# A gated linear attention block on one core: x rows at the head of the odd step, moments stored early, the second x split right behind the decays

## What is computed

```python
x = x + attention(layernorm(x))          # 16 heads of 64
x = x + (layernorm(x) @ CB.T) * (SCB / 127) + bias

# attention: q = elu(x Wq) + 1, k = elu(x Wk) + 1, v = x Wv, a = sigmoid(x Wa + ba + 2)
# per head, token after token:
S = a_t * S + outer(k_t, v_t);  z = a_t * z + k_t
out_t = (q_t @ S) / (q_t @ z + eps)      # then out @ Wo
```

## Time and profile before

| | |
|---|---|
| median of 3 runs | 2289.2 us (2288.9 to 2291.93) |
| the profiled execution | 2286.59 us, its span 2284.8 us |
| mean granted TensorE clock | 0.960 of full |
| PE busy | 2097.7 us (92% of the span) |
| DVE, ACT, POOL busy | 1457.7, 679.5, 307.7 us |

### The profile page before, as it was taken

How to read it: one execution, slowest core, us unless ns; L and a number is a source line. 1 busy time by engine, 2 the same in 40 slices (tenths; PEclk the granted TensorE clock), 3 DMA queues, 4 the chain that set the end, 5 groups by cost and what they waited for, 6 DMA issues and landing times. The chain is left out here.

```text
span 2284.8 us, 71079 instructions
## 1 busy us (share of the span) xinstructions
PE 2097.7 (92%) x28424; PEld 1800.9 (79%) x28424; DVE 1457.7 (64%) x3308; ACT 679.5 (30%) x1288; POOL 307.7 (13%) x367
## 2 busy tenths in 40 slices
PE   6898898899999998899999998999879999999999
PEld 5777787778888887788888887888768888888887
DVE  6566666676666766666667666666655555555554
ACT  4233333333333333333333333333421111111111
POOL 0121111111221111111211111112010000000000
PEclk9999999999999999999999999999989999999999
DMA  5323233333323233223222333233333333333332
GB/s 167 85 81 84 79 94 97 90 84 88 92 79 83 83 92 107 82 86 90 84 81 81 87 94 102 83 88 98 106 120 111 110 112 119 113 115 110 110 111 87
DMA packets 204592, 220.81 MB, mean 97 GB/s; under 512 B 31360, under 2 KB 146560, under 8 KB 204544
## 3 DMA queue, kind: packets, MB, share of 16 engines
q1 hardware_dynamic: 204544, 220.13, 31.6%
HBM read 168.59 MB, written 51.44 MB: 96 GB/s over the span
## 5 line engine op out<-in xcount | busy, mean ns | idle before, releaser
L1188 PE MATMUL G<-w_hi,xT_hi 128*128 128x512 f32 x1024 | 417.9, 408 | 6.0 <-DVE xT_lo L818 4.6
L1188 PE MATMUL G<-w_lo,xT_hi 128*128 128x512 f32 x1024 | 408.1, 399 | 0.0
L1188 PE MATMUL G<-w_hi,xT_lo 128*128 128x512 f32 x1024 | 405.3, 396 | 0.0
L1188 PE MATMUL G<-xT_hi,w_hi 128*128 128x256 f32 x1024 | 292.0, 285 | 28.4 <-DVE xT_lo L818 27.3
L1188 PE MATMUL G<-xT_lo,w_hi 128*128 128x256 f32 x1024 | 289.7, 283 | 0.0
L1188 PE MATMUL G<-xT_hi,w_lo 128*128 128x256 f32 x1024 | 289.7, 283 | 0.0
L682 ACT ACTIVATE relu_t<-G 128x512 f32<-128x512 f32 x256 | 152.7, 596 | 456.7 <-PE G L1188 456.7
L1188 PEld LDWEIGHTS G<-w_hi,xT_hi 128*128 128x128 f32 x1024 | 198.5, 194 | 50.5 <-DVE xT_lo L818 5.0
L1188 PEld LDWEIGHTS G<-w_hi,xT_lo 128*128 128x128 f32 x1024 | 197.3, 193 | 43.7
L1188 PEld LDWEIGHTS G<-xT_hi,w_hi 128*128 128x128 f32 x1024 | 196.1, 191 | 42.3 <-issue 41.1
L1188 PEld LDWEIGHTS G<-w_lo,xT_hi 128*128 128x128 f32 x1024 | 198.7, 194 | 36.9
(11 more groups left out here) (131 smaller groups left out, 3744.9 us busy)
## 6 DMA issues: line engine op xcount, KB each, us to landing
abc<-decay_rows SPq DMA_DIRECT2D x256, 128.0 KB, 3.1
pbc<-product_rows SPq DMA_DIRECT2D x256, 128.0 KB, 3.0
attn_rows<-attn SPq DMA_DIRECT2D x512, 64.0 KB, 2.0
at_rows<-attn_rows SPq DMA_DIRECT2D x64, 512.0 KB, 3.3
xt<-in_x SPq DMA_DIRECT2D x64, 256.0 KB, 2.7
x_in<-in_x SPq DMA_DIRECT2D x64, 256.0 KB, 3.4
out_rows<-xt SPq DMA_DIRECT2D x64, 256.0 KB, 2.0
xT_in<-in_xT SPq DMA_DIRECT2D x31, 512.0 KB, 5.0
```

The costliest lines, as they stand in the source:

```text
L1188: made = nc.tensor.matmul(to, lhs, rhs, start=(n == 0), stop=(n == len(passes) - 1))
```

## The change

On SP, `load_pair` is cut in two. `load_rows` (the two `xt` loads) stands at the head of the odd step, behind the first `abc` loads. `load_columns` (the `xT_in` load) stands behind the second `abc` loads of the odd step and ahead of the `pbc` loads. `spread_norm` is cut as well: `store_norm` stands at the head of the even step, and the rest of it (`bias_b`) ahead of the even step's `pbc` loads, with no wait between them but the store's own. On DVE, `x_lo(1)` stands right behind `decays()`, and `elu_k(1, 0)` ahead of `normalised(0)`, in both steps. In the written-out steps -1 and 0 the split of the fourth and fifth weight slabs (`split_hi(3)`, `split_lo(3)`, `split_lo(4)`), `chunk_decay`, and the first `x_stats` and `x_moments` change places.

```diff
-                def load_pair():
+                def load_rows():
 
                     for s in range(2):
                         later = row(sp, i + 3 + s)
...
                         sp.dma_start(xt[s][:, :], x_rows[bass.ds(later, C), :]).then_inc(x_loaded[s], 16)
+
+                def load_columns():
+
                     sp.wait_ge(xT_lo_ready[1], pairs[1])
                     sp.wait_ge(z_ready, pairs[1])
                     at = (pair + 2) * DM
...
+                def store_norm():
+
+                    sp.wait_ge(rstd_ready, pairs[1])
+                    sp.dma_start(norm_rows, moments[:, :, :].rearrange("p s a -> p (s a)")).then_inc(norm_stored, 16)
+
                 def spread_norm():
 
-                    sp.wait_ge(rstd_ready, pairs[1])
+                    sp.wait_ge(norm_stored, p16[0])
                     wait(sp, xT_normal, pairs[-1])
-                    sp.dma_start(norm_rows, moments[:, :, :].rearrange("p s a -> p (s a)")).then_inc(norm_stored, 16)
-                    sp.wait_ge(norm_stored, p16[0])
...
+                gates = b == 1 and exists(i + 1)
+                second = isinstance(i, int) and i == 0
                 if isinstance(i, int) and i == NC - 3:
                     output_weights()
+                if b == 0 and exists(i + 2) and not second:
+                    store_norm()
                 if exists(i):
                     spread_decays(1, this)
                 if b == 0 and exists(i + 1):
                     spread_decays(0, coming)
+                if b == 1 and exists(i + 3):
+                    load_rows()
                 if exists(i - 2):
                     store_rows(1, i - 2, one[-2])
-                if b == 1 and exists(i + 1):
+                if gates:
                     store_decays()
                     if not exists(i):
                         sp.wait_ge(w_lo_ready, KT)
                     spread_decays(0, coming)
...
+                    if exists(i + 3):
+                        load_columns()
+                if b == 0 and exists(i + 2):
+                    if second:
+                        store_norm()
+                    spread_norm()
...
                     spread_products(1, this)
                 if exists(i + 1):
                     spread_products(0, coming)
-                if b == 0 and exists(i + 2):
-                    spread_norm()
                 if exists(i - 1):
                     store_rows(0, i - 1, one[-1])
-                if b == 1 and exists(i + 3):
-                    load_pair()
...
                     q_parts(0)
+                    if not first:
+                        chunk_decay()
+                    q_parts(1)
                     if first:
                         split_hi(3)
-                    chunk_decay()
-                    q_parts(1)
+                        chunk_decay()
                     copy_v(0)
...
                 if gates and not first:
                     x_lo(0, pairs[1], xT_in[:, :, tokens(0)])
                     decays()
+                if second:
+                    x_stats(x16[1])
+                    dve.wait_ge(stats_ready, pairs[1])
+                    x_moments(pairs[1])
+                    split_lo(4)
+                if exists(i):
+                    if gates:
+                        x_lo(1, pairs[1], xT_in[:, :, tokens(1)])
+                    elu_k(1, 0)
                 if exists(i - 1):
                     normalised(0)
...
-                if second:
-                    split_lo(4)
                 if exists(i):
-                    elu_k(1, 0)
-                    if gates:
-                        x_lo(1, pairs[1], xT_in[:, :, tokens(1)])
                     decay_matrix(1)
...
                     elu_q(0, 0)
-                    if first:
-                        split_lo(3)
                     decay_matrix(0)
...
                     elu_q(1, 1)
+                    if first:
+                        split_lo(3)
```

More of the change, by code:

```diff
@@ L497, in step @@
                     spread_decays(0, coming)
-                wait(sp, qs_ready[1], one[-1] if exists(i - 1) else None)
-                wait(sp, qs_ready[0], one[0] if exists(i) else None)
-                wait(sp, pc_ready, one[0] if exists(i) else None)
+                    if exists(i + 3):
[4 more added lines that the diff above has]
+                    spread_norm()
+                if exists(i - 1):
+                    sp.wait_ge(qs_ready[1], one[-1])
                 if exists(i):
+                    sp.wait_ge(qs_ready[0], one[0])
+                    sp.wait_ge(pc_ready, one[0])
                     spread_products(1, this)
@@ L1060, in step @@
                     decay_matrix(0)
-                    if second:
-                        x_stats(x16[1])
-                        dve.wait_ge(stats_ready, pairs[1])
                     elu_q(3, 0)
-                    if second:
-                        x_moments(pairs[1])
                     elu_k(0, 1)
```

## The result

The changed kernel takes 2186.48 us (median of 4 runs, 2181.32 to 2187.88), the one before 2290.27 us on the same chip: a ratio of 0.954, 95% interval 0.9525 to 0.956. The forecast was 2178 us, inside whose range of 2138 to 2232 this lies; it came out 8.5 us short of the promised gain. The profiled execution is 2187.04 us, its span 2185.2; mean granted clock 0.989 instead of 0.960.

What follows compares the result with a forecast made beforehand. PE, 92% busy, was bound by waits on DVE, late because xt came late, and a low clock; 103.6 us from 28 pairs, 3.3 early and 3.8 prologue make 110.7 off 2286.6, plus 2.6 to the median: 2178, range 2138 to 2232.

Steps and rivals of the forecast that it cites:

- The sum: Even and odd step together: 45.2 us without waits plus 2.25 of waits, a pair of 47.5, 3.7 less than 51.2.
- `xt` at the head of the odd step: SP's two xt issues stand some 20 us earlier; DVE's 4.81 us idle goes, and q is bound by ACT's exp.
- The clock: Loop pairs: with 2.25 us in two smaller waits the granted clock stays 1.00, winning 1.8 us a pair.
- the rival of the low clock: Loop: the clock drops all the same, 1.8 us in each of 28 pairs come back, 2228 us; chance 0.13.
- kT ends last: Next even step's head: ACT's kT, not DVE's q, ends last; PE waits 1.5 us (1.2 to 1.95).
- The state wait: Even step's head, after the scores: state there at 862.05 us, PE ready at 861.3, a wait of 0.75.
- `xT_in` ahead of `pbc`: SP's odd step: the load delays pbc by 0.95 us, 0.65 of issue and 0.3 of bytes (0.65 to 1.4).
- The rival in which `pbc` stands behind all of the 512 KB: SP, after the decays: the DMA queue works on 512 KB first, pbc lands 4 us late, 2316 us; slower, chance 0.05.
- `x_lo(1)` behind the decays: DVE ends xT_lo by 846.4 us, before PE needs it at 847.26; PE's wait of 0.92 us is won.
- Moments earlier: POOL's operations move some 10 us ahead; PE's first-pair wait of 6.27 us goes, weight splits lose 2.5, prologue wins 3.8.
- that rival: DVE's even step: POOL's operations slow it until q or k is late, 1 us a pair, 2206 us; chance 0.05.
- The early pairs and the tail: Outside the steady loop: two early pairs, without low clock, gain 1.6 us each; other pairs counted at the loop's 3.7.

Runs made afterwards that it cites:

- e2: The kernel before, with only the two xt loads moved to the head of the odd step: 2156.93 us, ratio 0.9426.
- e7b: The changed kernel with xT_in's load behind the odd step's last stores and an unused 2 KB load in its old place: 2164.28 us, ratio 0.9452.
- e3: The changed kernel with x_lo(1) and k on DVE put back behind the normalisation: 2174.53 us, ratio 0.9501.
- e5b: The kernel before, with only x_lo(1) and k on DVE moved ahead of the normalisation: 2297.11 us, ratio 1.0029.
- e8b: The kernel before, with only the change's reordering on ACT and DVE in the written-out steps -1 and 0: 2285.02 us, ratio 0.9976.
- e4: The changed kernel with the moments stored and loaded back behind the even step's pbc loads: 2184.05 us, ratio 0.9548.
- the 13 kernels: The kernel before, the changed kernel, and all follow-up variants of either; profiled spans from 2117.0 to 2294.8 us.
- after: The changed kernel itself, with all parts of the change, against the kernel before: 2186.48 us, ratio 0.954.
- e1: The changed kernel with xT_in's load put back to the end of SP's odd step, behind pbc: 2146.43 us, ratio 0.9375.

## Why the prediction was right, and where it wasn't

**The sum.** The loop pair was forecast at 47.5 us and is 47.47. That is better than its terms deserve: by the means over the 26 pairs the waits are 1.65 + 1.24 = 2.89 us, not 2.25, and the pair without them is 44.6 us, not 45.2. The two errors of 0.6 us cancel, which is luck.

**`xt` at the head of the odd step.** Right, and it is the whole gain of the loop: e2 with this part alone has 4.80 us a pair. The long idle of DVE is gone, q waits for exp, and the head's waits shrink.

**The clock.** Right in the loop, whose granted clock is 1.00. As means over the 26 pairs, the even step less its two waits was 27.41 - 2.37 - 1.17 = 23.87 us and is 24.85 - 2.89 = 21.96: 1.9 us, near the 1.8 read from two even steps. Before, the clock fell in each of the 26 pairs (0.93 or 0.97 of full over the pair); after, in one, that of step 38, with waits of 1.99 and 0.46 us, while the pair of step 30 kept 1.00 with 2.12 and 1.27. So the waits alone do not say when it falls. In the pairs 4-5 and 6-7, and in step 62, the low clock came after all, behind waits of 3.07, 3.18 and 3.33 us: there the rival of the low clock was right.

**kT ends last.** Right in kind and size: 1.50 us of wait forecast, 1.50 measured in the pair shown and 1.65 as the mean over the loop, put down to ACT's kT. Both inputs were a little off: `pbc` came 1.06 us later (0.95 forecast) and ACT took 856.10 + 1.09 - 854.53 = 2.66 us behind pc, not 3.1.

**The state wait.** Mis-sized: 0.75 forecast, 1.28 measured (1.24 as the mean). From q's start to the end of the state are 859.35 + 0.86 - 855.92 = 4.29 us, exactly as forecast, so that chain was sized right. Against pc, q started 0.19 us later than taken (855.92 - 854.53 = 1.39, not 1.2), and ACT's chain was 0.44 us shorter, so PE came to the place where it waits for the state that much sooner. The two make 0.63, about the difference of 0.53.

**`xT_in` ahead of `pbc`.** The mechanism was right, a size was off. The issue was taken at 0.65 and costs 0.65 (e7b); the bytes were taken at 0.3 and cost 0.60. Together 1.25 us a pair, within the bounds of 0.65 to 1.4. This is the part of the change that makes the loop slower, 33 us over 26 pairs. The rival in which `pbc` stands behind all of the 512 KB has its mechanism in part and not its price: `pbc` landed 4.0 us after its issue instead of the 3.0 measured for the same load before, and not 4 us later.
The Trainium skill (DMA: Bandwidth & Descriptors, Queues, rings and completion order) says that descriptors are consumed in ring order on each DMA engine. The trace agrees in kind, with 0.60 us; the prediction's estimate of 1.2 us from that page's fit of 436 GB/s, all of it on the path, is twice what e7b leaves for the bytes. The page gives that fit for DMAs issued from GpSimd, and here SP issues them.

**`x_lo(1)` behind the decays: the step that failed.** "0.92 us won" is wrong as a gain: e3 and e5b show nothing for it in the loop, in either kernel. PE doesn't end a step with it, it only comes sooner to a wait whose end is set by ACT or DVE. The prediction itself worked out the head's waits from PE's arrival "0.92 earlier", so the loss was in the 1.50 us and the sum stayed right; only the account of which edit earns what was wrong. By that account, undoing this edit, with the move of k beside it that was taken as nothing, would have cost 0.9 us a pair. It costs nothing in the loop and makes the whole kernel 12 us faster (e3). The edits of `x_lo(1)` and of k were not run apart, so which of them costs the 12 us is open.

**Moments earlier.** "The wait of 6.27 us goes", and 3.8 us in the prologue: 4.1 were measured, but by another cause. e8b has most of them, 3.5, without the early store, and e4 without the early store too; they come from what the change does to the order of steps -1 and 0 on ACT and DVE, which the forecast had put at 2.5 us lost. The early store is worth 0.14 us a pair.
POOL's operations are slower beside DVE (1221 ns against 981), and DVE's D scan is too, 1.89 us against 1.22; none of it lies on PE's path, so that rival fell.

**The early pairs and the tail.** Here the 8.5 us are. Forecast were 1.6 us for each of the pairs 2-3 and 4-5, and 3.7 for 6-7 and 60-61, 10.7 in all; measured were -0.1, -0.1, 1.2, and 3.4 us lost from step 60 on. That is 10.7 + 2.4 = 13.1 us less than forecast. The prologue and the 26 pairs gave 0.3 + 1.7 more, so the profiled execution came out 11 us above its forecast of 2175.9; the median is 8.5 above, since it lies 0.6 under that execution and not over it. The pair 60-61 itself gained 3.2 us; steps 62 and 63 lost 3.8 and what follows them 2.9, in a stretch where the 13 kernels differ by 3.1 among themselves. I carried the loop's gain into single pairs, and in these DVE's new order brings waits of its own, on a store up to 2 us later than in the loop, and with them the low clock. Without it, in e3, the pairs 2-3, 4-5 and 6-7 gain 1.4, 1.9 and 4.5 us, and the kernel takes 2174.5 us, 3.5 under the forecast.

## What to carry to other kernels

A wait that comes back once a loop has a price only if nothing behind it waits for something else: before counting it as won, ask when the next wait's releaser ends in absolute time, and take away the earlier one only together with the later. Put loads that are not urgent where the issuing queue would otherwise stand idle, not ahead of a small load that an engine waits for; the issue alone was half of what it cost here. And on an engine that works in order, fill its wait for another engine with the small work that stands behind it, rather than leaving that work between the wait and the result that others need: this was worth 1.0 us a pair, with a few lines moved. Last, an edit that shows nothing in the loop can still cost in the written-out steps around it: run each part by itself and compare whole kernels, not loops alone.

## What the runs showed of the hardware

- A load of 512 KB issued ahead of smaller, urgent ones on SP cost 1.25 us a pair; 0.65 of it with 2 KB in its place (after, e1, e7b). The issue was as dear as the bytes.
- POOL's tensor operations took 1221 ns beside DVE's even step and 981 elsewhere (means, after and e4), and DVE's scan of 128x512 took 1.89 us instead of 1.22 when it started while one of them ran. POOL's began at 867.56 us, behind the first scan's start and ahead of the second's:

```profile
867.33 1.22 DVE L1018 TENSOR_TENSOR_SCAN D<-abc,eye 128x512 f32<-128x512 f32 x1
...
871.81 1.89 DVE L1018 TENSOR_TENSOR_SCAN D<-abc,eye 128x512 f32<-128x512 f32 x1
```

The Trainium skill (SBUF — State Buffer, Who interferes with whom) says that a DVE instruction with two SBUF inputs contends with a GpSimd instruction that reads SBUF, and that the ports they share are an exclusive lock. The trace agrees, and shows who loses: of the 52 scans in the 26 pairs that overlapped an operation of POOL, the 26 that had started ahead of it took 1.22 us, and the 26 that started while one ran took 1.89, 55% more.

- At the turn of the loop DVE stood 0.87 us between two operations for no releaser that the profile shows, and 0.35 us when it had less to do just ahead of it.
- With DVE's new order a store of 8 KB in steps 3, 5 and 61 held SP for 2.1 to 3.1 us instead of 1.0, in all nine kernels that have it and in none of the four that don't. One transfer in the instruction queue lay in each of these waits of after and in none of e3's.
- The granted clock fell from 2.4 to 1.2 GHz for a part of each of the 26 pairs before, behind waits of 2.2 to 2.9 us before the scores, and in one of 26 after the change, whose waits there were 1.4 to 2.1 us.
